# Two attention leads: projections in halves of 256 columns dealt between maxima, placing in rounds by term, mask casts on GpSimd

## What is computed

```python
q = proj(wq, bq); k = proj(wk, bk); v = proj(wv, bv)
q = q * cos + _rotate_half(q) * sin
k = k * cos + _rotate_half(k) * sin
scores = jnp.einsum('bhqd,bhkd->bhqk', q, k) * scale
attn = jax.nn.softmax(scores, axis=-1)
out = jnp.einsum('bhqk,bhkd->bhqd', attn, v)
```

## Time and profile before

| | |
|---|---|
| median of three runs | 2094.41 us (2093.96 to 2098.53) |
| profiled execution | 2091.26 us |
| its span, first to last instruction | 2089.2 us |
| mean granted TensorE clock | 0.927 |
| PE, DVE, ACT, POOL busy | 89%, 74%, 66%, 17% of the span |
| maxima on VectorE (L787) | x832, 907.4 us |

### The profile page before, as it was taken

How to read it: one execution, slowest core, us unless ns; L and a number is a source line. 1 busy time by engine, 2 the same in 40 slices (tenths; PEclk the granted TensorE clock), 3 DMA queues, 4 the chain that set the end, 5 groups by cost and what they waited for, 6 DMA issues and landing times. The chain is left out here.

```text
span 2089.2 us, 40754 instructions
## 1 busy us (share of the span) xinstructions
PE 1853.3 (89%) x16072; PEld 929.9 (45%) x16072; DVE 1550.8 (74%) x2264; ACT 1382.2 (66%) x2565; POOL 365.2 (17%) x522
## 2 busy tenths in 40 slices
PE   6799999999999686748998999999778999999785
PEld 2122222222223286714676776767612333334385
DVE  6899999999996332435787677787578989876434
ACT  3499999999998332325554556666346898888431
POOL 4201000000002322142442122121241000000213
PEclk8699999999999798869999999999877999999798
DMA  5000000000000367500000000000100000000174
GB/s 167 1 3 4 5 9 4 9 5 5 10 7 4 115 219 225 180 20 0 1 1 1 1 1 1 1 1 1 53 0 1 4 5 11 5 12 6 49 262 155
DMA packets 53021, 81.70 MB, mean 39 GB/s; under 512 B 9216, under 2 KB 37888, under 8 KB 52704
## 3 DMA queue, kind: packets, MB, share of 16 engines
q1 hardware_dynamic: 47664, 70.63, 10.8%
q0 software_dynamic: 3072, 6.30, 1.0%
q10 hardware_dynamic: 2096, 2.17, 0.4%
HBM read 64.26 MB, written 12.06 MB: 37 GB/s over the span
## 5 line engine op out<-in xcount | busy, mean ns | idle before, releaser
L787 DVE TENSOR_REDUCE a_mx<-psum 128x2 f32<-128x1024 f32 (+2 forms) x832 | 907.4, 1160 | 79.7 <-PE psum L559 42.6
L713 ACT ACTIVATE a_cs<-psum 128x512 f32<-128x512 f32 (+3 forms) x1664 | 858.3, 571 | 95.4 <-PE psum L528 35.7
L603 PE MATMUL psum<-a_cs,a_V 128*16 128x256 f32 (+1 forms) x6400 | 503.6, 386 | 12.7 <-ACT a_OD L693 8.8
L559 PE MATMUL psum<-a_KS,a_QS 48*128 48x512 bf16 (+3 forms) x1664 | 328.5, 385 | 31.4 <-DVE a_mx L787 28.5
L578 PE MATMUL psum<-a_QS,a_KS 51*128 51x512 bf16 (+3 forms) x1664 | 340.8, 379 | 15.4 <-issue 7.5
L2083 PE MATMUL psum<-b_VW,b_ST 128*128 128x129 f32 x2176 | 252.6, 277 | 12.9 <-DVE X L2193 12.9
L2083 PEld LDWEIGHTS psum<-b_VW,b_ST 128*128 128x128 f32 x2176 | 248.6, 194 | 14.6 <-DVE X L2193 14.6
L578 PEld LDWEIGHTS psum<-a_QS,a_KS 51*128 51x128 bf16 x1664 | 88.5, 93 | 367.2 <-ACT a_cs L713 315.8
L2064 PE MATMUL psum<-b_GT,AT 128*128 128x512 f32 (+3 forms) x640 | 243.1, 534 | 1.6 <-ACT b_ST L2119 1.6
L603 PEld LDWEIGHTS psum<-a_cs,a_V 128*16 128x16 f32 x6400 | 107.3, 94 | 232.0 <-issue 121.0
L2168 DVE TENSOR_TENSOR b_M<-b_M,b_ST 128x512 f32<-128x512 f32 (+3 forms) x288 | 174.9, 607 | 42.6 <-ACT b_ST L2119 12.8
(11 more groups left out here) (227 smaller groups left out, 1536.8 us busy)
## 6 DMA issues: line engine op xcount, KB each, us to landing
e_W<-in_l_experts SPq DMA_DIRECT2D x45, 576.0 KB
e_W<-in_l_experts SPq DMA_DIRECT2D x21, 768.0 KB, 5.9
yg<-e_yout SPq DMA_DIRECT2D x14, 256.0 KB
xg<-zeros SPq DMA_DIRECT2D x2, 1472.0 KB, 9.5
a_cs<-in_rope ACTq DMA_DIRECT2D x4, 512.0 KB, 9.9
a_QS<-a_mrow SPq DMA_DIRECT2D x128, 3.0 KB
a_cs<-in_rope SPq DMA_DIRECT2D x1, 2048.0 KB, 7.9
a_num<-a_OD SPq DMA_DIRECT2D x120, 16.0 KB
```

The lines of the kernel that those rows point to most:

```text
L559: mm = pe.matmul(ps[:, 2 * slot + half, 0:width], QS[rows, 2 * p + i, q_cols(qb, qt * P, P)], KS[rows, 2 * p + i, c * BLK:c * BLK + width] ...
L603: mm = pe.matmul(ps[32 * j:32 * j + 2 * HD, AV_BANK, a:b], V[:, kt, HPP * p + j, :], probs(e, a, b), start=(kt == 0 and half == 0), stop=last,
L713: act.activation(probs(HPP * s + j, c, BLK), ps[:, plan.bank(entry), c:BLK], ACT.Exp, scale=scale).then_inc(exp_done, 1)
L787: dve.tensor_reduce(mx[:, pk % 2, qt, 2 * i:2 * i + 2, c], banks, AX.X, ALU.max).then_inc(max_done, 1)
```

## The change

Three things change in the lead, none in the numbers computed.

- Operands from 4 on (`WHOLE`) are projected and turned in halves of 256 columns, so ring items are ("project", s, j, h).
- `Plan.lead_order` writes the order of each loop. From loop 2 on it deals one maximum behind every token: half projection, half projection, the three rounds of set 0, two half projections, the three rounds of set 1. A round (`place_term`) is the four matmuls of one term. In loop 1 set 0 of operand 1 comes first, then the first projection of operand 3, set 1, the second projection. VectorE's order follows the same list.
- The mask casts move from VectorE to GpSimd, after the low split of operand 4, and the four small GpSimd instructions for pack 0 (`maxima(0)`) from behind the last low split to ahead of it.

```diff
--- before.py
+++ after.py
@@ -104,6 +104,7 @@
 SETS = ((0, 2, 4, 6), (1, 3, 5, 7))
 NU = 2 * len(SETS)
 EARLY = 2
+WHOLE = 4
...
-        self.ring = [("project", s, j) for s in range(2) for j in range(2)]
-        for s, mine in enumerate(self.lead):
-            if s + 2 < len(self.operands):
-                self.ring += [("project", s + 2, 0)] + mine[:1] + [("project", s + 2, 1)] + mine[1:]
-            else:
-                self.ring += mine
+        self.opened = [("project", s, j, 0) for s in range(2) for j in range(2)]
+        self.order_of_lead = [self.lead_order(s, mine) for s, mine in enumerate(self.lead)]
+        self.ring = self.opened + [item for row in self.order_of_lead for item in row if item[0] != "set"]
         self.ring += [item for row in self.halves for item in row if item[0] == "scores"]
         self.number = {}
         for n, item in enumerate(self.ring):
@@ -186,6 +184,36 @@
         lead[2 + NB] += left[:half]
         lead[3 + NB] += left[half:]
         return lead
+
+    def parts(self, s):
+
+        return 1 if s < WHOLE else 2
+
+    def turned(self, s, j, h):
+
+        return sum(2 * self.parts(a) for a in range(s)) + self.parts(s) * j + h + 1
+
+    def lead_order(self, s, mine):
+
+        ahead = [("project", s + 2, j, h) for j in range(2) for h in range(self.parts(s + 2))] if s + 2 < len(self.operands) else []
+        first, second = ([("set", v, t) for t in range(TERMS)] for v in range(2))
+        if s == 0:
+            return ahead + first + second
+        if s == 1:
+            return first + ahead[:1] + second + ahead[1:]
+        out, left = [], list(mine)
+
+        def deal(group):
+            for token in group:
+                out.append(token)
+                if left:
+                    out.append(left.pop(0))
+
+        deal(ahead[:len(ahead) // 2])
+        deal(first)
+        deal(ahead[len(ahead) // 2:])
+        deal(second)
+        return out + left
...
+                for s in range(NOP):
+                    split_rest(s)
+                    if s == 3 + plan.chunks(order[0]):
+                        maxima(0)
+                    if s + 1 < NOP:
+                        rotate(s + 1)
+                    split_low(s)
+                    if opening and s == NB:
+                        opening.cast_masks(pool)
+                pool.wait_ge(consts_set, 3)
+                for pk in range(NPK):
+                    if pk:
+                        maxima(pk)
...
-                def project(s, j):
+                def project(s, j, h):
                     which, n = plan.operands[s]
+                    wide = BLK // plan.parts(s)
                     if s < 2 and j == 0:
                         pe.wait_ge(*arrived[which])
-                    if "x" in arrived and j == 0:
+                    if "x" in arrived and j == 0 and h == 0:
                         pe.wait_ge(*arrived["x"][n])
-                    slot = slot_of(("project", s, j))
-                    pe.matmul(ps[:, 2 * slot, :], w["w" + which + "r" * j][:, :], src_T[:, n * BLK:(n + 1) * BLK],
+                    slot = slot_of(("project", s, j, h))
+                    a = n * BLK + h * wide
+                    pe.matmul(ps[:, 2 * slot, 0:wide], w["w" + which + "r" * j][:, :], src_T[:, a:a + wide],
                               start=True, stop=True).then_inc(max_ready, 1)
 
                 def values(g):
@@ -502,23 +540,23 @@
                                        w["wv"][:, :], start=True, stop=True)
                     mm.then_inc(v_ready, 1)
 
-                def place_set(s, v):
+                def place_term(s, v, t):
                     which = 0 if plan.operands[s][0] == "k" else 1
-                    if v == 0:
+                    if v == 0 and t == 0:
                         pe.wait_ge(low, s + 1)
-                    if v:
+                    if v and t == 0:
                         wait_copies(pe, s, 2 * v - 1)
-                    elif s:
+                    elif s and t == 0:
                         wait_copies(pe, s - 1, NU - 1)
-                    else:
+                    elif t == 0:
                         pe.wait_ge(v_done, NB)
-                    for t in range(TERMS):
-                        for i, u in enumerate(SETS[v]):
-                            rows = slice(32 * i, 32 * (i + 1))
-                            mm = pe.matmul(ps[:, 4 + i, :], place[rows, which, t, u, :],
-                                           terms[rows, s % 2, t, :], start=(t == 0), stop=(t == TERMS - 1))
-                            if t == TERMS - 1 and i % 2:
-                                mm.then_inc(place_ready, 1)
+                    for i, u in enumerate(SETS[v]):
+                        rows = slice(32 * i, 32 * (i + 1))
+                        mm = pe.matmul(ps[:, 4 + i, :], place[rows, which, t, u, :],
+                                       terms[rows, s % 2, t, :], start=(t == 0), stop=(t == TERMS - 1),
+                                       skip_group_check=True)
+                        if t == TERMS - 1 and i % 2:
+                            mm.then_inc(place_ready, 1)
...
-                    mine = plan.lead[s]
-                    half = (len(mine) + 1) // 2
-                    if s + 2 < NOP:
-                        project(s + 2, 0)
-                    for item in mine[:1]:
-                        max_item(item)
-                    if s + 2 < NOP:
-                        project(s + 2, 1)
-                    place_set(s, 0)
-                    for item in mine[1:half]:
-                        max_item(item)
-                    place_set(s, 1)
-                    for item in mine[max(1, half):]:
-                        max_item(item)
+                    for item in plan.order_of_lead[s]:
+                        if item[0] == "project":
+                            project(*item[1:])
+                        elif item[0] == "set":
+                            place_term(s, item[1], item[2])
+                        else:
+                            max_item(item)
...
-                    src, by = ps[:, 2 * (k % 2), :], cs[:, j, n * BLK:(n + 1) * BLK]
+                    name = "b" + which + "r" * j
+                    t = (t1, t2)[j][:, s % 2, h * wide:(h + 1) * wide]
+                    src, by = ps[:, 2 * (k % 2), 0:wide], cs[:, j, n * BLK + h * wide:n * BLK + (h + 1) * wide]
...
-                    mine = plan.lead[s]
-                    if s + 2 < NOP:
-                        turn(s + 2, 0)
-                    for item in mine[:1]:
-                        max_item(item)
-                    if s + 2 < NOP:
-                        turn(s + 2, 1)
-                    for v in range(NU):
-                        if plan.by_vector(s, v):
-                            evacuate(s, v)
-                    if opening and s == 1:
-                        opening.cast_masks(dve)
-                    for item in mine[1:]:
-                        max_item(item)
+                    for item in plan.order_of_lead[s]:
+                        if item[0] == "project":
+                            turn(*item[1:])
+                        elif item[0] != "set":
+                            max_item(item)
+                        elif item[2] == TERMS - 1 and plan.by_vector(s, 2 * item[1] + 1):
+                            evacuate(s, 2 * item[1] + 1)
...
-    def cast_masks(self, dve):
+    def cast_masks(self, pool):
         core = self.core
-        dve.wait_ge(self.ident_in, 16)
-        dve.wait_ge(self.masks_in, 48)
-        dve.tensor_copy(core.identb[:, :], core.ident[:, :]).then_inc(self.cast, 1)
+        pool.wait_ge(self.ident_in, 16)
+        pool.wait_ge(self.masks_in, 48)
+        pool.tensor_copy(core.identb[:, :], core.ident[:, :]).then_inc(self.cast, 1)
         for i, dst in enumerate((core.ident2, core.neg2, core.neg2t)):
-            dve.tensor_copy(dst[:, :, :], self.stage[:, i, :, :]).then_inc(self.cast, 1)
+            pool.tensor_copy(dst[:, :, :], self.stage[:, i, :, :]).then_inc(self.cast, 1)
```

28 lines of the change are left out of this document (11 added, 17 removed).

## The result

| | before | after |
|---|---|---|
| median of nine runs each | 2094.81 us (2092.27 to 2098.66) | 2102.75 us (2101.25 to 2109.53) |
| profiled execution | 2091.26 us | 2109.53 us |
| its span | 2089.2 us | 2107.2 us |
| mean granted TensorE clock | 0.927 | 0.918 |

The ratio is 1.0043, 95% interval 1.003 to 1.0057: the change costs 0.43%, some 8 to 9 us. The profiled execution of the changed kernel is the slowest of its nine, so its span shows 18.0 us more; the leads hold 10.6 of that, as the table further down says.

The account below looks back on a forecast made before the run. Both leads were taken to move the end directly, without slack behind them. Terms -5.1 + 1.4 + 3.5 + 2.5 + 3.4 - 2.65 + 0.4 gave about +3.5 us: 2097.9 us against the median, range 2086 to 2106.

Parts of the forecast that it names:

- The low-clock rival: Both leads: TensorE stays at 1.2 GHz throughout, all terms at the low level; +7.7 us, 2102.1 us; chance 0.28.
- What bounds the kernel: Both leads: no engine is full there, the stages behind have no slack, so a lead's shift moves the end equally.
- Halves between maxima: First lead, loops 2 to 5: half projections and half turns bring a loop from 13.90 to 12.4 us; -5.1 us.
- The start: Up to operand 4's first half turn, which waits for a low split: +1.4 us first lead, +3.5 us second.
- Mask casts and pack 0: GpSimd's casts and four small maxima in their new places: cost 0; possible gains up to 2.3 and 0.6 us.
- The tail: Loops 6 and 7: rounds alternate with maxima, sets wait for ScalarE's copies; +2.5 us first lead, +3.4 us second.
- the all-high sum of -11.8: All terms with TensorE at its high clock level, the starts at +0.6 and +2.2 us: -11.8 us.
- The crossing's wait: Start of loop 6: its round needs copies of the set just finished; VectorE waits 2.6 us low, 1.3 high.
- Second lead, loops 2 to 5: Second attention: three loops gain, -2.65 us; loop 5, whose short maxima cover no half projection, +0.4 us.
- The new first wait: Rival: the low split comes late in every loop, six loops losing some 2 us; 2100 to 2104 us; chance 0.10.
- the even order would keep TensorE at 2.4 GHz: Rival, both leads: high clock from the new order; -11.8 us in full, 2082.6 us; chance 0.25.

## Why the prediction was right, and where not

The forecast was 2097.9 us, the measurement 2102.75: inside the range of 2086 to 2106, and slower by more than 0.2%, to which the text gave the largest chance (0.39). But its own number, +3.5 us, is less than half of the 8 measured, and stood within that 0.2%. The low-clock rival had 2102.1. So the direction and the places of gain and loss were right by working, while the hit of a range 20 us wide with a forecast that was too small is in part luck: nearly every term erred to the same side, none by more than 2 us. Step by step:

- **What bounds the kernel.** Right. A lead that ends later moves the end; the second kernel part behind it takes no slack (from the second memset on, 346.9 us before and 347.1 to the same statistics after).
- **Halves between maxima.** Right: a half projection 1.22 us low and 0.70 high (1.2 and 0.6 taken), a half turn 0.48, a loop 12.45 (12.4). The share of the high level was right too: the first lead's loops were granted 0.66, which is one third of the time at 2.4 GHz. At the low level alone a loop is 12.96 us in the kernel with the old loop 1 (predicted 12.75), at the high one 11.4 (11.65). But the halves are not what brings most of it: with whole sets they gain 1.0 us in the four loops, and the rounds between maxima the other 3.4. The Trainium skill ("VectorE: DVE Perf Modes", section on the TRN2 errata) tells to keep tiles at 512 elements or more. A fixed cost per instruction is in the trace, 0.21 us for two halves; it was paid, and the loops gained all the same.
- **The start.** The mechanism was right: the rows of 35.24 and 1540.27 are both released by the low split, and the old loop 1 takes the loss back. The term of the first lead, +1.4, measured +2.4. The step that failed is "Copy 1.0, second set 1.5, then only the second projection of operand 3": it leaves out the first projection of operand 3, which the new order puts between the two sets on TensorE. That projection took 2.08 us, ended 0.5 us behind ScalarE's copy, and the second set started at 29.10 where the sum has 27.9. In the second lead it is the same (projection 1531.98 to 1534.05, ScalarE's copy done at 1533.55, second set at 1533.99). The first set also started at 25.69 and not at 24.7, and ScalarE's copy did not move to 26.9 (27.65; before 27.64), because operand 0's second set took 1.47 us. The 0.83 that the sum relied on belongs to one execution of the kernel before: in twelve of the fourteen traces that set took 1.07 to 1.47 us. Together the turn of operand 3 ran at 31.91 instead of 31.0. In the second lead the +3.5 measured +3.1.
- **Mask casts and pack 0.** Both 0, as said: ratio 0.9995 for the first; for the second the first tail unchanged, in one trace.
- **The tail.** The step that failed in size. "Three rounds and two maxima of TensorE, 2.3 us low" took 2.83, since each step of the alternation costs 0.54 us at the low level, where I had taken 0.43 for a round from the row of a whole set. So 4.83 from set to set where 4.4 was said, three times, is +1.3 of the +1.8 missing; the rest lies in the crossing (2.9 instead of 2.75), the last maxima, and the 0.2 taken off for some time at the high level, of which there was none (0.50). The other end of this term, 17.1 us at the high level, doesn't come out of its own parts (1.45 + 3 x 3.4 + 4.6 = 16.2); the forecast doesn't rest on it, but the all-high sum of -11.8 does. The crossing's wait itself was foreseen (2.6, measured 2.68 and 2.72). What was not seen is that it belongs to loop 5's rounds: with the tail whole again it stays, and only an earlier last set removes it.
- **Second lead, loops 2 to 5.** The sizes failed by the level: "one third of the time at the high level" didn't hold where the lead was granted 0.57. Loops 2 to 4 gave 1.5 us instead of 2.65: 38.3 us, the 3 x 12.75 of the low level. Loop 5 took 12.26 at a granted 0.50 instead of 10.9, above even the low end of 11.85; its short maxima cover neither the half projection nor the 0.54 us steps. At a granted 0.99 the same loop takes 8.86 us (version with the old loop 1), close to the 9.1 said for the high level.

The rivals. That TensorE stays at 1.2 GHz throughout both leads came about in part: 0.50 in both tails and 0.57 in the second lead's loops, but 0.66 in the first lead's loops, as before the change (0.67). Its price of +7.7 us is close to the 8 us measured, but its condition held only in part, so that is no proof of it. Nor is the clock alone why the change is slower: taking back start and tail, with a granted 0.60 and 0.56 in the loops and 0.50 in the first tail, gives 0.9975. The new first wait did not repeat: from loop 3 on VectorE waits for TensorE alone. That the even order would keep TensorE at 2.4 GHz fell: from 58 to 72 us TensorE's rows fill 13.47 of 14.00 us, and the granted clock is 0.50. The Trainium skill ("TensorE: Matmul & The Clock Gate", part on what is happening) says that activity releases the throttled state, and I counted that for this rival. By that rule the change should have been lifted, and the trace does not bear it out: 44.64 us of matmul rows in 46 us were granted 0.50 in the changed kernel with maxima twice, while 10.48 of 14 us were granted 1.00 in the version with maxima twice in the loops. A matmul's row is longer at the low level, so these shares don't measure the same work; what they show is that rows without gaps did not bring the high level here.

What is shown: the start and the tail together turn a gain of 0.25% into a loss of 0.43%. Of the two alone, the start shows in the time (1.0007 with it taken back) and the tail does not (1.0035); on top of the restored start the tail does (0.9975). Not shown: why the clock takes one level or the other in a given order.

**Versions that beat both kernels.** The change with the old loop 1 and the old tail (0.9975), the same with the last set of loop 5 early (0.9971), that with the second lead in its old order (0.9968), and those with maxima twice: in the tail (0.9972), in the loops as well (0.9938, in one session), and in the kernel before (0.9974). Between them the intervals tell little; only the 0.9938 stands somewhat apart. The one with the last set early is the one to keep: it adds no work and both tails are short. The 0.9938 rests on a clock that the same doubling in another setting did not get (1.0122).

## What to carry to other kernels

Dealing small pieces of producer work between the consumer's pieces pays where the consumer starves at long pieces (here 1.4 us per loop, most of it by the rounds). It costs where a third engine drains in whole sets: there a set should be finished early, so that its copies run beside other work. Before moving a step, list what stands ahead of it on every queue it touches, its own engine's first: here a projection of 2.08 us on TensorE between two sets was left out of the sum, and the start came 2.4 us later instead of 1.4. And before resting a term on a row, see whether other executions have it: a set of 0.83 us was 1.07 to 1.47 in nearly all of them.

## What the runs showed of the hardware

- Rounds of four matmuls (32 rows) and pairs of a maximum (48 rows) in alternation are 0.54 us apart at the low level each, though twelve such matmuls in one piece take 1.47 us: the 0.43 per round of the sum was too small by a fifth.
- TensorE's rows can fill 44.64 of 46 us and the granted clock still be 0.50 (38 to 84 us, changed kernel with maxima twice), and a stretch with 10.48 of 14 us filled can run at 1.00 (46 to 60 us, maxima twice in the loops).
- Work added for nothing changed the granted clock of a tail from 0.50 to 0.80 and shortened nothing. Added in the loops as well, it moved the ratio from 0.9972 to 0.9938 in one setting; added to the change, it moved it from 1.0043 to 1.0122.
- Of the three casts of 128x256 on VectorE two took 0.29 us (31.23 and 31.43 us, before), and the third, beside a GpSimd instruction of 31.54 to 32.73, took 1.24. On GpSimd, with VectorE at its maxima, each takes 0.41 us (59.48, changed kernel).
